# Probabilities times V in smaller steps: one key tile per step, one step per slot, starting a slot earlier

## The chip, the cores and the metric

The kernel runs on one core of a Trainium2 chip. The metric is the device time of one execution in microseconds (us); it is given as the median of three runs. The engines are TensorE (PE, with its weight loads listed apart as PEld), VectorE (DVE), ScalarE (ACT), GpSimd (POOL) and the DMA queues, which SyncE (SP) mostly issues.

## What is computed

Eight sequences of 256 tokens with 128 features pass through four attentions and three feed-forward blocks. Cut to what matters here:

```
x += tanh(g) * attention0(layernorm(x), ctx, ctx)      # 512 keys, 16 heads of 8
x += tanh(g) * moe0(layernorm(x))                      # 8 experts, top 1
z  = layernorm(x)
y  = ln(z + attention1(z, z, z))                       # 256 keys
y  = ln(y + attention2(y, ctx, ctx))                   # 512 keys
y  = ln(y + relu(y @ fc1) @ fc2);  x += tanh(g) * y
u  = x + attention3(rms(x))                            # 256 keys, causal, rope
x += tanh(g) * (u-block: u + moe1(rms(u)))             # 4 experts, top 2
attention:  S = Q K^T * scale;  P = softmax(S);  O = P V   for 16 heads of each of 8 sequences
```

## The kernel before, in words

There are 32 attention batches n (attention 0 for eight sequences, then 1, 2 and 3, named att0 to att3). An attention batch is cut into slots: 16 for 512 keys (one head each, `kt` = 4 key tiles of 128), 8 for 256 keys (two heads each, `kt` = 2). Four heads make a group, so a group is 4 slots (`gs`) with 512 keys and 2 slots with 256.

In a slot TensorE does, in this order, the step E (the transposed scores of the slot's heads with the row maxima folded in, four matmuls, L1654, which ScalarE turns into probabilities by exp, two instructions of 512 columns, L1098, in a ring of nine buffers), and the units S (plain scores of a head some slots ahead, L1619 for 512 keys, L1633 for 256, L1627/L1629 in att3; VectorE takes their maxima, L1288, L1297, L1293). Most slots have two S units; some of att3's have one. Between the S units stand the small products (MISC: q, k, v, transposes "maxT", "ctx", "aT", "proj", "nT") and, in later att0 and early att1 batches, the tiles of the first mixture of experts (L1753, L1762).

The step AV multiplies a group's probabilities with V: per key tile and head one matmul with 128 rows and 32 columns of the array (L1670); four heads fill the four column strips and accumulate in one PSUM bank, `av_ps`. In the trace one such fp32 matmul is two instructions, so 8 matmuls are x16. After a group's last AV step ScalarE copies the bank out (L1102, tile OT), and only then may the next group's first step begin; the first step also waits for the exp of the group's last slot. The same bank serves the second fully connected layer `f.down` (L1783, copied out at L1171), four times in the program.

The order is fixed when the program is built: `body` lists the steps of a batch slot by slot, every engine walks the same list and does its own part. `avs` is how many AV steps a group has. In a slot the AV step is put before the last S unit. Each PE step waits only for what it needs, in order, so whatever stands behind a waiting step waits too. PSUM: three banks for E, three for S (two with 256 keys), the rest for the small products; which step takes which bank is worked out from the same list.

Of the kernel before, what the change touches and what calls it, by code (L numbers as in the profile page):

```python
# [26 lines left out]
NG = HEADS // GH  # L27
# [22 lines left out]
class Att:  # L50
# [3 lines left out]
    def __init__(self, name, keys, own_kv, rope, wo, tail):  # L54
        self.name, self.keys, self.own_kv, self.rope, self.wo, self.tail = name, keys, own_kv, rope, wo, tail
        self.kt = keys // P
        self.slots = HEADS * self.kt * SQ // 1024
        self.hps = HEADS // self.slots
        self.gs = self.slots // NG
        self.lead = 2 * self.gs + 1  # L60
        self.avs = self.kt // 2

    def units(self, s):

# [14 lines left out]
def att(n):  # L79
    return ATTS[n // B]  # L80


def run_of(n):
    return next((lo, hi) for lo, hi in RUNS if lo <= n < hi)
# [9 lines left out]
def post_items(n):  # L94

    a = att(n)
    if n < B and n % HALF == HALF - 1:
        return {4: [("ctx", n, 0)], 5: [("ctx", n, 1)], 6: [("aT", n, None)], 7: [("proj", n, None)],
                9: [("apply", n, None)], 10: [("nT", n, None)]}
    it = {6: [("ctx", n, 0)], 7: [("ctx", n, 1)], 15: [("nT", n, None)]}  # L100
    if a.wo:
        it[8] = [("aT", n, None)]
        it[10 if a.rope else 11] = [("proj", n, None)]
        it[12 if a.rope else 14] = [("apply", n, None)]
    else:
        it[8] = [("resid", n, None)]
        it[10] = [("center", n, None)]
        it[13] = [("apply", n, None)]
    return it


def s_units(n, s, u):

    out = [("S", n, (s, u))]
    a = att(n)
    gs = a.gs
    if u == a.units(s) - 1 and s % gs == gs - 1:
        out.append(("maxsplit", n, s // gs))
    return out
# [170 lines left out]
def opens_half(n):  # L290

    return B <= n < 2 * B and n % HALF == 0
# [12 lines left out]
def body(n, plan):  # L305

    a = att(n)
    lo, hi = run_of(n)
    items = {p: [] for p in range(16)}

    def put(p, *steps):
        items[p] += list(steps)

    put(1, ("maxT", n, 1))
    if n + 1 < hi:
        for hf in range(QUARTERS):
            put((3, 4, 7, 11)[hf] if opens_half(n + 1) else PARTS_AT[hf], ("loadqk", n + 1, hf))
    if n > lo:
        put(2, ("loadres", n - 1, None))
    put(4 if a.rope else 5, ("maxT", n, 2))  # L320
    put(8 if a.rope else 9, ("maxT", n, 3))
    if n + 1 < hi:
        put(13, ("maxT", n + 1, 0))
    if n + 2 < hi and not opens_half(n + 2):
        if n + 2 < 2 * B:
            put(0, ("xapply", n + 2, None))
            put(1, ("xT", n + 2, None))
            if n + 2 >= B:
                put(2, ("xstore", n + 2, None))
        long_k = att(n + 2).kt > 2  # L330
        put(2, ("q", n + 2, None), ("qsplit", n + 2, None))
        put(4, ("k", n + 2, None), ("ksplit", n + 2, 0))
        put(5, ("qstore", n + 2, None))
        if long_k:
            put(6, ("ksplit", n + 2, 1))
        put(10 if long_k else 9, ("kstore", n + 2, None))
    if n > lo:
        for p, st in post_items(n - 1).items():
            put(p, *st)
    if n + 1 < hi:  # L340
        put(12 if a.rope else 10, ("v", n + 1, None))
    if n + 3 < hi:
        if n + 3 < 2 * B and not (n + 3 >= B and (n + 3) % HALF < 2):
            put(8, ("loadx", n + 3, None))
            put(14, ("xstat", n + 3, None))
        if not B <= n + 3 < 2 * B:
            put(12, ("loadin", n + 3, None))
    for k in range(2):
        if 0 <= 2 * (n - WEIGHTS_AT) + k < 2 + 3 * E1:
            put((6, 12)[k], ("weights", n, 2 * (n - WEIGHTS_AT) + k))  # L350
    for p in range(16):
        put(p, *MOE0_ITEMS.get((n, p), ()))
        put(p, *FFN_ITEMS.get((n, p), ()))
    out = []
    per = 16 // a.slots
    for s in range(a.slots):
        ahead = [(m, t, u) for m, t in plan[(n, s)] for u in range(att(m).units(t))]
        units = [s_units(*x) for x in ahead]
        product = []
        if s >= a.gs:  # L360
            product = [("AV", n, (s // a.gs - 1, x)) for x in range(a.avs) if (x + 1) * a.gs // a.avs - 1 == s % a.gs]
        elif n > lo:
            p = att(n - 1)
            product = [("AV", n - 1, (NG - 1, x)) for x in range(p.avs) if (x + 1) * a.gs // p.avs - 1 == s]
        if product:
            units.insert(max(1, len(units) - 1), product)
        tiles = TILE_ITEMS.get((n, s), [])
        units[1:1] = [[st] for st in tiles if st[0] == "m0.h"]
        chunks = [[]]
        for p in range(per * s, per * s + per):  # L370
            for st in items[p] + [st for st in tiles if st[0] != "m0.h" and p % per == per - 1]:
                if st[0] in MISC_KINDS:
                    chunks.append([])
                chunks[-1].append(st)
        out.append(("E", n, s))
        out += weave(units, chunks)
    return out


def weave(units, chunks):  # L380


    rest = chunks[1:]
    if not units:
        units = [[]]
    last, gaps = len(units) - 1, max(1, len(rest) - 1)
    out = list(chunks[0])
    for k, unit in enumerate(units):
        out += unit
        for i, chunk in enumerate(rest):  # L390
            if (2 * i * last + gaps) // (2 * gaps) == k:
                out += chunk
    return out
# [41 lines left out]
def all_steps():  # L435
    out = []
    for lo, hi in RUNS:
        plan = s_plan(lo, hi)
        out += start_steps(plan)
        for n in range(lo, hi):  # L440
            out += body(n, plan)
    return out + moe1_steps()
# [1445 lines left out]
```

## Time and profile before

| | us |
|---|---|
| median of 3 runs | 1217.94 (1216.9 to 1221.68) |
| the profiled execution | 1213.76 |
| its span in the trace | 1211.9 |
| PE busy / DVE busy / ACT busy | 1058.7 / 791.5 / 617.9 |
| mean granted clock of TensorE | 0.941 of full speed |

The span is what the trace covers; about 1.9 us of the profiled execution lie outside it. Busy times of PE are modelled from overlapping matmuls, so that a busy PE may still have short gaps in what it streams; the start times of neighbouring matmuls show these.

### The profile page before, as it was taken

Reading aid. Unit: us, or ns where it says so; the run is one execution under the profiler, and the core shown is the slowest. Engines: PE = TensorE matmul, PEld = TensorE weight load, DVE = VectorE, ACT = ScalarE, POOL = GpSimd, SP = SyncE. Lnnn points to the kernel's source line nnn. Section 1 sums busy time; section 2 is a strip of 40 time slices with the busy share of each in tenths; the row PEclk is TensorE's granted clock in tenths of the full one; section 3 lists DMA queues with packets and bytes.
Section 4 is the critical chain, followed back from the end, with each engine's and each line's share of the span. In section 5 each row is a group of like instructions: output and inputs, shape, how many; then the busy total and the mean of one; then the engine's idle time right before and its main releaser. Section 6 shows DMA issues by size and latency. Waiting matters only on the chain. (4 is left out here: it accounts for less than half of the span.)

```text
span 1211.9 us, 25281 instructions
## 1 busy us (share of the span) xinstructions
PE 1058.7 (87%) x8548; PEld 653.8 (54%) x8548; DVE 791.5 (65%) x1935; ACT 617.9 (51%) x1331; POOL 368.3 (30%) x982
## 2 busy tenths in 40 slices
PE   3999997899887678789799998897989899899998
PEld 1355554576554566445455544444556567656665
DVE  3788888635877213577688869679674766645443
ACT  1477765555663433465477765655644444543221
POOL 3433333221445112542433334213242434200000
PEclk9999999999996788788899998999988989999999
DMA  7556644553444442554666553633434355201000
GB/s 196 157 169 177 174 143 142 183 182 97 126 132 143 155 127 86 161 158 149 212 180 179 151 165 96 179 96 106 123 111 131 115 162 166 88 27 33 20 24 13
DMA packets 173877, 158.76 MB, mean 131 GB/s; under 512 B 13011, under 2 KB 147539, under 8 KB 173395
## 3 DMA queue, kind: packets, MB, share of 16 engines
q1 hardware_dynamic: 169558, 142.03, 39.7%
q0 software_dynamic: 4192, 15.12, 3.9%
q8 instruction: 70, 1.15, 0.4%
q14 instruction: 57, 0.47, 0.1%
HBM read 91.56 MB, written 67.63 MB: 131 GB/s over the span
## 5 line engine op out<-in xcount | busy, mean ns | idle before, releaser
L1098 ACT ACTIVATE prob<-ps 128x512 f32<-128x512 f32 (+1 forms) x768 | 399.3, 579 | 166.1 <-PE ps L1654 123.2
L1288 DVE TENSOR_REDUCE nmax<-ps 128x1 f32<-128x512 f32 x512 | 328.0, 682 | 82.8 <-PE ps L1619 80.6
L1654 PE MATMUL ps<-Qst,Kst 75*128 75x256 bf16 x1408 | 241.6, 282 | 5.9 <-DMA Qst<-mrow 3.0
L1619 PE MATMUL ps<-Kst,Qst 72*128 72x512 bf16 x512 | 195.8, 398 | 24.4 <-DVE nmax L1288 20.8
L1670 PE MATMUL av_ps<-prob,Vx 128*32 128x256 f32 (+1 forms) x3072 | 216.0, 398 | 0.0
L1654 PEld LDWEIGHTS ps<-Qst,Kst 75*128 75x128 bf16 x1408 | 135.7, 100 | 70.8 <-ACT prob L1098 11.5
L1670 PEld LDWEIGHTS av_ps<-prob,Vx 128*32 128x32 f32 x3072 | 92.3, 114 | 66.9 <-issue 37.6
L1020 POOL TENSOR_TENSOR mparts<-nmax,zeros 128x8 bf16<-128x8 f32 x122 | 24.5, 201 | 328.2 <-issue 320.4
L1297 DVE TENSOR_REDUCE nmax<-ps 128x2 f32<-128x512 f32 x128 | 85.7, 686 | 47.3 <-PE ps L1633 46.6
L1102 ACT ACTIVATE OT<-av_ps 128x256 f32<-128x256 f32 x128 | 49.2, 384 | 113.6 <-PE av_ps L1670 113.1
L1619 PEld LDWEIGHTS ps<-Kst,Qst 72*128 72x128 bf16 x512 | 50.2, 99 | 104.7 <-DVE nmax L1288 51.0
L1293 DVE TENSOR_REDUCE nmax<-ps 128x2 f32<-128x512 f32 (+1 forms) x96 | 65.4, 685 | 38.5 <-PE ps L1629 37.7
L1184 ACT ACTIVATE prob<-ps 128x512 f32<-128x512 f32 x48 | 28.7, 597 | 87.2 <-PE ps L1808 87.1
L1633 PE MATMUL ps<-Kst,Qst 72*128 72x256 bf16 x256 | 55.7, 303 | 15.6 <-DVE nmax L1297 11.5
L1159 ACT ACTIVATE m_hid<-ps,wbig 128x256 f32<-128x256 f32 x88 | 35.7, 472 | 57.4 <-PE ps L1762 32.2
L1753 PE MATMUL ps<-FB,wbig 128*128 128x256 f32 x176 | 49.6, 431 | 13.4 <-DMA wbig<-in_w,widx 13.3
L1130 ACT ACTIVATE mrow<-ps 12x256 bf16<-12x256 bf16 x128 | 46.5, 363 | 28.0 <-PE ps L1701 26.2
L1487 DVE TENSOR_TENSOR FB<-ps,wbig 128x256 f32<-128x256 f32 x22 | 9.3, 424 | 75.0 <-PE ps L1762 75.0
L1627 PE MATMUL ps<-Kst,Qst 72*128 72x128 bf16 (+1 forms) x256 | 49.9, 259 | 6.1 <-DVE nmax L1293 6.0
L1570 DVE SCALAR_TENSOR_TENSOR FB<-ps,comb,FB 128x128 f32<-128x128 f32 x64 | 18.0, 344 | 53.9 <-PE ps L1815 53.9
L1815 PEld LDWEIGHTS ps<-wbig,prob 128*128 128x128 f32 x384 | 45.2, 192 | 9.4 <-issue 9.4
L1753 PEld LDWEIGHTS ps<-FB,wbig 128*128 128x128 f32 x176 | 36.1, 216 | 20.7 <-DMA wbig<-in_w,widx 13.9
(198 smaller groups left out, 1673.6 us busy)
## 6 DMA issues: line engine op xcount, KB each, us to landing
k_parts<-kp SPq DMA_DIRECT2D x48, 384.0 KB, 3.4
q_parts<-qp SPq DMA_DIRECT2D x96, 192.0 KB, 2.6
Qst<-q_parts SPq DMA_DIRECT2D x128, 144.0 KB
Kst<-k_parts SPq DMA_DIRECT2D x64, 288.0 KB
k_parts<-kp SPq DMA_DIRECT2D x48, 192.0 KB, 2.6
Kst<-k_parts SPq DMA_DIRECT2D x64, 144.0 KB
ctxT<-in_ctxT SPq DMA_DIRECT2D x16, 256.0 KB, 5.1
xs_rows<-in_blank SPq DMA_DIRECT2D x22, 128.0 KB, 4.0
```

The costliest lines, as they stand in the source:

```text
L1098: act.activation(prob[:, RING_AT[st] % RING, half * 512:half * 512 + w], bank(x)[:, 0:w], ACT.Exp).then_inc(drained(x), 1)
L1102: act.activation(OT[:, n % 2, arg[0], :], av_ps[:, 0:SQ], ACT.Copy).then_inc(av_drained, 1)
L1130: act.activation(mrow[:, arg % 2, :], bank(st)[0:PARTS * GH, :].bitcast(BF16)[:, 0:SQ], ACT.Copy) \
L1288: ve.tensor_reduce(nmax[:, g, u, h % GH:h % GH + 1], bank(st), AX.X, ALU.max, negate=True).then_inc(drained(st), 1)
L1293: ve.tensor_reduce(dst, bank(st).rearrange("p (h k) -> p h k", h=2 if k else GH), AX.X, ALU.max, negate=True).then_inc(drained(st), 1)
L1297: ve.tensor_reduce(nmax[:, g, :, h % GH:h % GH + 1], bank(st).rearrange("p (t k) -> p t k", t=QT), AX.X, ALU.max, negate=True).then_inc(dr ...
L1619: last = pe.matmul(bank(st), Qst[0:ROWS, par, s, u * P:u * P + P], Ks[0:ROWS, par, s, :], start=True, stop=True)
L1627: pe.matmul(o, Qst[0:ROWS, par, h, t * P:t * P + P], Ks[0:ROWS, par, h, 0:w], start=True, stop=False)
L1633: last = pe.matmul(bank(st)[:, t * SQ:t * SQ + SQ], Qst[0:ROWS, par, h, t * P:t * P + P], Ks[0:ROWS, par, h, 0:SQ], start=True, stop=True)
L1654: last = pe.matmul(o, Ks[0:KROWS, par, h, t * P:t * P + P], Qst[0:KROWS, par, h, :], start=True, stop=not a.rope)
L1670: last = pe.matmul(av_ps[VW * hh:VW * hh + VW, SQ - w:SQ], Vx[:, par, t, h, :], prob[:, place, off * SQ:off * SQ + w], start=(t == 0), sto ...
L1753: last = pe.matmul(bank(x)[:, u * TILE:(u + 1) * TILE], w_0[:, arg % WRING, t * P:t * P + P], xs_T[:, arg % 2, :], start=True, stop=True)
```

## The change

Each group has one AV step per key tile (`avs` is `kt` instead of `kt // 2`), with 4 matmuls instead of 8. The rule that places them is rounded up instead of down: the steps of a group with 512 keys stand in the four slots behind the group's last (before: in the second and the fourth of them), with 256 keys in both slots behind it (before: in the second). The last step stays in the slot where it was. The matmuls are the same, 1536 in the program; what stands between them differs. Where an attention with 256 keys follows one with 512, the four steps of the last group stand two and two together.

```diff
@@ class Att
-        self.avs = self.kt // 2
+        self.avs = self.kt
@@ body
         if s >= a.gs:
-            product = [("AV", n, (s // a.gs - 1, x)) for x in range(a.avs) if (x + 1) * a.gs // a.avs - 1 == s % a.gs]
+            product = [("AV", n, (s // a.gs - 1, x)) for x in range(a.avs) if -(-(x + 1) * a.gs // a.avs) - 1 == s % a.gs]
         elif n > lo:
             p = att(n - 1)
-            product = [("AV", n - 1, (NG - 1, x)) for x in range(p.avs) if (x + 1) * a.gs // p.avs - 1 == s]
+            product = [("AV", n - 1, (NG - 1, x)) for x in range(p.avs) if -(-(x + 1) * a.gs // p.avs) - 1 == s]
```

TensorE's order in an att2 batch (slots 1 to 3 of batch 17), before. L1654 is E, L1619 is S, L1670 is AV, L1701 is maxT, L1687 is q:

```order
L1619 MATMUL ps<-Kst,Qst 128x512
L1701 MATMUL ps<-identb,mparts 12x128 x2
L1670 MATMUL av_ps<-prob,Vx 32x256 x8
L1619 MATMUL ps<-Kst,Qst 128x512
L1654 MATMUL ps<-Qst,Kst 128x256 x4
L1619 MATMUL ps<-Kst,Qst 128x512
L1687 MATMUL ps<-inT,wts 128x256
L1619 MATMUL ps<-Kst,Qst 128x512
L1654 MATMUL ps<-Qst,Kst 128x256 x4
L1619 MATMUL ps<-Kst,Qst 128x512
L1670 MATMUL av_ps<-prob,Vx 32x256 x8
```

The same slots on the same engine now:

```order
L1619 MATMUL ps<-Kst,Qst 128x512
L1701 MATMUL ps<-identb,mparts 12x128 x2
L1670 MATMUL av_ps<-prob,Vx 32x256 x4
L1619 MATMUL ps<-Kst,Qst 128x512
L1654 MATMUL ps<-Qst,Kst 128x256 x4
L1619 MATMUL ps<-Kst,Qst 128x512
L1687 MATMUL ps<-inT,wts 128x256
L1670 MATMUL av_ps<-prob,Vx 32x256 x4
L1619 MATMUL ps<-Kst,Qst 128x512
L1654 MATMUL ps<-Qst,Kst 128x256 x4
L1619 MATMUL ps<-Kst,Qst 128x512
L1670 MATMUL av_ps<-prob,Vx 32x256 x4
```

Slot 2 has an AV step of its own, and each step is half as long. Over the program the AV matmuls stand in 379 unbroken runs instead of 192.

TensorE's order around `f.down` (L1783) in batch 19, before:

```order
L1670 MATMUL av_ps<-prob,Vx 32x256 x8
L1619 MATMUL ps<-Kst,Qst 128x512
L1654 MATMUL ps<-Qst,Kst 128x256 x4
L1783 MATMUL av_ps<-prob,wbig 128x512 x4
L1619 MATMUL ps<-Kst,Qst 128x512 x2
L1654 MATMUL ps<-Qst,Kst 128x256 x4
L1619 MATMUL ps<-Kst,Qst 128x512
L1701 MATMUL ps<-identb,mparts 12x128 x2
L1670 MATMUL av_ps<-prob,Vx 32x256 x8
```

The same place now:

```order
L1670 MATMUL av_ps<-prob,Vx 32x256 x4
L1619 MATMUL ps<-Kst,Qst 128x512
L1654 MATMUL ps<-Qst,Kst 128x256 x4
L1783 MATMUL av_ps<-prob,wbig 128x512 x4
L1619 MATMUL ps<-Kst,Qst 128x512
L1670 MATMUL av_ps<-prob,Vx 32x256 x4
L1619 MATMUL ps<-Kst,Qst 128x512
L1654 MATMUL ps<-Qst,Kst 128x256 x4
L1619 MATMUL ps<-Kst,Qst 128x512
L1701 MATMUL ps<-identb,mparts 12x128 x2
L1670 MATMUL av_ps<-prob,Vx 32x256 x4
```

An AV step, which writes the bank that `f.down` has just filled, stands one S unit behind it; before, a whole slot lay between them. The orders of DVE, ACT, POOL and SP are the same row for row, their semaphore waits included.

## Rows read from the trace of the kernel before

**Rows 1.** The page: busy time of each engine; TensorE's granted clock in 40 slices.

```profile
PE 1058.7 (87%) x8548; PEld 653.8 (54%) x8548; DVE 791.5 (65%) x1935; ACT 617.9 (51%) x1331; POOL 368.3 (30%) x982
...
PEclk9999999999996788788899998999988989999999
```

**Rows 2.** Windows: busy us (count) of PE, PEld, DVE, ACT, POOL; clock; DMA.

```profile
42.20:164.70 122.50, 117.18 (x1021) 65.51 (x1019) 103.08 (x231) 85.64 (x178) 44.63 (x128) 1.00 0.58 171
244.00:283.00 39.00, 37.78 (x277) 29.38 (x275) 12.18 (x22) 20.94 (x52) 6.48 (x10) 1.00 0.54 170
...
493.00:613.00 120.00, 98.69 (x777) 55.18 (x776) 84.55 (x197) 63.51 (x139) 48.82 (x135) 0.84 0.61 181
613.00:696.10 83.10, 81.02 (x748) 45.15 (x747) 72.98 (x148) 62.19 (x130) 30.98 (x90) 1.00 0.56 167
...
733.80:770.30 36.50, 31.12 (x261) 16.89 (x259) 33.15 (x84) 21.66 (x44) 14.33 (x41) 0.91 0.47 141
...
885.40:1072.00 186.60, 166.29 (x1813) 120.82 (x1810) 123.05 (x350) 87.53 (x215) 68.33 (x211) 0.92 0.43 128
```

**Rows 3.** Waits in 613 to 696.1: who waited for whom, us, times, longest.

```profile
DVE nmax L1288 <- PE ps L1619: 7.6, 18, 0.8
...
PE ps L1619 <- DVE nmax L1288: 1.5, 6, 0.4
```

**Rows 4.** Timeline of TensorE in batch 17: start, us, what, xcount.

```profile
640.30 0.60 PE L1619 MATMUL ps<-Kst,Qst 72*128 72x512 bf16 x2
640.74 0.65 PE L1654 MATMUL ps<-Qst,Kst 75*128 75x256 bf16 x4
...
644.15 0.60 PE L1654 MATMUL ps<-Qst,Kst 75*128 75x256 bf16 x4
644.59 0.38 PE L1619 MATMUL ps<-Kst,Qst 72*128 72x512 bf16 x1
644.90 1.07 PE L1670 MATMUL av_ps<-prob,Vx 128*32 128x256 f32 x16
645.90 0.39 PE L1619 MATMUL ps<-Kst,Qst 72*128 72x512 bf16 x1
646.13 0.60 PE L1654 MATMUL ps<-Qst,Kst 75*128 75x256 bf16 x4
```

**Rows 5.** The page's groups: busy, mean ns, idle before them and its releaser.

```profile
L1288 DVE TENSOR_REDUCE nmax<-ps 128x1 f32<-128x512 f32 x512 | 328.0, 682 | 82.8 <-PE ps L1619 80.6
...
L1670 PE MATMUL av_ps<-prob,Vx 128*32 128x256 f32 (+1 forms) x3072 | 216.0, 398 | 0.0
...
L1670 PEld LDWEIGHTS av_ps<-prob,Vx 128*32 128x32 f32 x3072 | 92.3, 114 | 66.9 <-issue 37.6
...
L1619 PEld LDWEIGHTS ps<-Kst,Qst 72*128 72x128 bf16 x512 | 50.2, 99 | 104.7 <-DVE nmax L1288 51.0
```

**Rows 6.** Timeline of ACT in the same slots as rows 4.

```profile
644.94 1.09 ACT L1098 ACTIVATE prob<-ps 128x512 f32<-128x512 f32 x2 [0.17 <-ACT qk L1111]
646.03 0.38 ACT L1102 ACTIVATE OT<-av_ps 128x256 f32<-128x256 f32 x1
```

**Rows 7.** Timeline around the first `f.down`, all engines.

```profile
723.13 3.70 PE L1783 MATMUL av_ps<-prob,wbig 128*128 128x512 f32 x8 [0.37 <-ACT OT L1102]
...
726.66 0.60 PE L1619 MATMUL ps<-Kst,Qst 72*128 72x512 bf16 x2
...
726.86 0.69 ACT L1171 ACTIVATE FB<-av_ps,cols 128x512 f32<-128x512 f32 x1 [2.81 <-PE av_ps L1783]
...
727.08 1.89 DVE L1288 TENSOR_REDUCE nmax<-ps 128x1 f32<-128x512 f32 x3 [4.07 <-PE ps L1619]
```

**Rows 8.** Waits over the whole span.

```profile
DVE nmax L1288 <- PE ps L1619: 80.6, 87, 7.2
...
DVE nmax L1297 <- PE ps L1633: 46.6, 40, 5.3
...
DVE nmax L1293 <- PE ps L1629: 37.7, 42, 5.7
```

## The prediction, made before the changed kernel was run

> **What bounds the kernel now.** I read the busy times first. TensorE is busy 1058.7 of 1211.9 us, VectorE 791.5, ScalarE 617.9, GpSimd 368.3 [rows 1]. An average says little in a program of so many stages, so I cut it into windows [rows 2]. In the plain 512-key batches (42 to 164.7 and 613 to 696.1) TensorE is busy 117.2 of 122.5 and 81.0 of 83.1 us; in the tiles of the first experts (244 to 283) 37.8 of 39. In the 256-key batches it has more room: 98.7 of 120 (attention 1) and 166.3 of 186.6 (attention 3). Batch 20 (733.8 to 770.3) is VectorE's: 33.2 of 36.5 us against TensorE's 31.1.
>
> In the plain batches VectorE is close behind: 73.0 of 83.1 us. The waits tell which of the two is late. VectorE waited 7.6 us for scores, TensorE 1.5 us for a score bank to be read [rows 3]. So TensorE is what is late, by a little; both have almost no room.
>
> The timeline shows how a slot is made up [rows 4]. Two S matmuls take 0.60 us where one takes 0.38, so the next starts 0.22 us after the last. E begins at 644.15 and the S behind it at 644.59, 0.44 us. A slot without AV is thus 0.44 + 2 x 0.22 = 0.88 us of TensorE; the slot with AV, from E at 644.15 to E at 646.13, is 1.98. The mean of 1.43 stands against 2 x 0.682 = 1.36 us of VectorE's maxima [rows 5] plus its other work. Light and heavy slots alternate, and the three score banks even them out.
>
> **What an AV run costs.** S starts at 644.59 and AV at 644.90, 0.31 us later instead of 0.22: entering costs 0.09. The run of 16 instructions takes 1.07 us. They go four at a time, one per column strip, so it is one matmul's 0.38 us and three further rounds of (1.07 - 0.38) / 3 = 0.23. The next S starts 1.00 us after the run began, 0.07 before its last end [rows 4]. A run of 4 matmuls is two rounds: 0.38 + 0.23 = 0.61, less 0.07 is 0.54. With the entry, 8 matmuls in one run are 1.00 + 0.09 = 1.09 us and in two runs 2 x (0.54 + 0.09) = 1.26. Each further run costs 0.17 us at full clock.
>
> The Trainium skill speaks against the change at this place. "TensorE: Matmul & The Clock Gate", section "Part 3: Packing small matmuls — row/col tiling", says that a weight load overlaps running matmuls only if it goes to other row groups; AV takes all 128 rows and 32 columns, its neighbours all rows too. By that rule each further run would pay one load of either kind, 0.114 and 0.099 us [rows 5], 0.21 us and 39 us over the kernel; the trace agrees in kind, with 0.17.
>
> **The change part by part.** Matmuls, bytes and the other engines' orders stay. Every group with 512 keys has two more runs and every group with 256 keys one: 16 batches x 8 + 16 x 4 = 192, less 5 where two steps stand together (two in each of the two passages from 512 to 256 keys, one at the end). That is the 187 of 379 - 192. 187 x 0.17 = 31.8 us more of TensorE's time. What of it reaches the end depends on the stretch:
>
> - Plain batches 0 to 3, 7 and 16 to 18: 64 runs, 10.9 us. Their idle TensorE is 5.3 us in four batches and 2.1 in three [rows 2]. Some of that idle is S waiting for a bank in the slots that had no AV, and an AV step before it covers that wait. I take 7 tenths on the path: 7.6 us. Bounds 3 and 10.9.
> - Batches 5 and 6 with expert tiles: 16 runs, 2.7 us, little idle TensorE; 7 tenths, 1.9. Bounds 1 and 2.7.
> - Batches 19, 21 and 23 with the fully connected layers: 24 runs, 4.1 us. VectorE starves there (4.07 us before 727.08 [rows 7]), so TensorE sets the pace: 2.9. Bounds 2 and 4.1.
> - Batches 4, 20, 22: 24 runs, 4.1 us, VectorE's; nothing. Bounds 0 and 2.
> - The 256-key batches: 59 runs, 10.0 us. TensorE stands idle there 21.3 of 120 and 20.3 of 186.6 us; three tenths, 3.0. Bounds 0 and 7.
>
> **The new wait.** The first step of a group is one slot earlier and needs the exp of the slot before and the copy of `av_ps`. In batch 17 the last exp of slot 3 ends at 644.94 + 1.09 = 646.03 and the copy at 646.41 [rows 6]; the slot's E started at 646.13 and takes 0.44, so S starts at 646.57 and AV 0.31 later at 646.88: 0.47 us of room. With half the matmuls in slot 3 the copy is ready sooner, by up to 0.46, and TensorE also arrives sooner by the same. I take nothing; at 0.1 us for each of 128 groups it would be 13 us, a high bound that I find unlikely.
>
> Behind `f.down` there is no such room. Its copy runs 726.86 to 727.55; the S before starts at 726.66, so AV could start at 726.97 and must wait until about 727.6 [rows 7]. Queued behind it are the other S unit, which VectorE is starving for, and the next E, for which ScalarE is busy anyway. 0.65 x 4 = 2.6 us, bounds 0 and 4.
>
> **What evenness gives back.** A slot that was heavy loses 0.46 us between its two S units, so VectorE is fed more evenly. VectorE waited for scores 80.6, 46.6 and 37.7 us in all [rows 8], but much of it in expert tiles and `f.down`, which stay. In the plain batches it can't help beyond what I left off the path above. In the 256-key batches and in 4, 20 and 22 it can: I take about a tenth of the 84.3 us of L1297 and L1293, 8 us, bounds 0 and 25.
>
> Sum: 7.6 + 1.9 + 2.9 + 0 + 3.0 + 2.6 - 8 = 10 us. The profiled execution of 1213.76 would become 1223.8. The median of the runs shown stands 4.2 us higher, and I predict against it: 1217.94 + 10 = 1228.
>
> **Rivals.**
> - *Evenness wins.* Alternation of 0.88 and 1.98 us slots starves VectorE in every heavy slot: 18 waits in 83 us [rows 3]. If steady feeding takes 7.6 us down to 2 there and the same share elsewhere, with TensorE's own waits gone as well, up to 25 us come back in the 256-key batches and the plain ones lose only 3. Against it: a starved VectorE costs nothing while TensorE is late. It decides if TensorE's streaming in plain batches has more gaps than the 2.1 us seen. Time: 10 + 8 - 25 - 5 is -12, about 1206. Chance 0.17.
> - *It cancels.* The lower bounds of the costs (3 + 1 + 2) against 6 of the gain: 1218. Chance 0.2.
> - *Every run is on the path.* 31.8 + 2.6 and nothing given back: 1252. Needs TensorE to be the bound everywhere, against its 21.3 us idle in attention 1 [rows 2]. Chance 0.06.
> - *The clock moves.* From 493 to 613 the granted clock averages 0.84 and from 885.4 to 1072 0.92: about 38 and 30 us at 1.2 instead of 2.4 GHz. It falls there because TensorE waits in bursts. If AV work in the light slots keeps it up in half of these, up to half of 34 us comes back, and about 1211 is reached; if other gaps appear it may be lost the same way, 1240. Chance 0.07, half each way. The Trainium skill ("TensorE: Matmul & The Clock Gate", "Part 1: The HAM clock gate") says that the throttled state is the default and activity lifts it; taken alone it would favour the first half, and no row here shows AV's placing to move it.
> - *The forecast*, 1221 to 1240, chance 0.5.
>
> **How the numbers follow.** About 0.5% (6 us) is what a measurement of this kernel can tell from no change. Faster: 0.17 and 0.02 of the clock, 0.19. Same: 0.2 of cancelling and 0.06 of the forecast's lower edge, 0.26. Slower: the rest, 0.55. The range of 1209 to 1243 takes in cancelling, the mild part of evenness and the bounds of the costs; outside lie the strong win below and the all-on-path case above, together about 2 in 10. The forecast's own range is 1221 to 1240.
>
> **What would show it.** The changed kernel's timeline of a plain slot should show each slot near 1.5 us instead of 0.9 and 2.0; S to AV 0.31 and AV run of x8 with the next S 0.54 after its start. Batches 16 to 18 should take about 3 us more than 83.1. VectorE's waits for L1619 should be shorter and more frequent. Behind `f.down` a wait of L1670 on ACT of about 0.6 us should stand four times. The prediction is wrong if the plain batches get shorter, if x8 runs follow each other without the 0.17 us, or if att1 and att3 shrink by more than 8 us.

## The result, and the profile after

| | before | after |
|---|---|---|
| median | 1218.18 us (5 runs) | 1251.42 us (5 runs) |
| the same comparison again, beside the experiments | 1221.32 us (17 runs) | 1246.75 us (6 runs) |

The ratio is 1.0235 with an interval of 1.0172 to 1.0298, and 1.0284 (1.0198 to 1.0371) the second time. The medians are of all executions; the ratios leave out those that stand more than 1.5% above the fastest of their kernel. The change makes the kernel 2 to 3% slower. The direction was forecast; 1228 us and the range up to 1243 were too low. The profiled execution has a span of 1243.2 us, 31.3 more than before.

The page of the changed kernel, answering to [rows 1] and [rows 5]:

```profile
PE 1103.0 (89%) x8548; PEld 635.7 (51%) x8548; DVE 798.0 (64%) x1935; ACT 621.7 (50%) x1331; POOL 368.4 (30%) x982
...
PEclk9999997899997889887799998898997999899999
...
L1288 DVE TENSOR_REDUCE nmax<-ps 128x1 f32<-128x512 f32 x512 | 332.2, 685 | 104.0 <-PE ps L1619 102.5
L1670 PE MATMUL av_ps<-prob,Vx 128*32 128x256 f32 (+1 forms) x3072 | 259.5, 404 | 3.7 <-ACT FB L1171 2.7
```

The matmuls are as many as before, and TensorE is busy 44 us longer, all but a little of it at L1670 (259.5 against 216.0 us). VectorE waits 22 us more for the scores of the long attentions in this pair of traces, although they come more evenly. The granted clock averages 0.924 instead of 0.941.

TensorE's timeline of batch 17, answering to [rows 4]:

```profile
655.84 0.60 PE L1654 MATMUL ps<-Qst,Kst 75*128 75x256 bf16 x4
656.28 0.38 PE L1619 MATMUL ps<-Kst,Qst 72*128 72x512 bf16 x1
656.59 0.64 PE L1670 MATMUL av_ps<-prob,Vx 128*32 128x256 f32 x8
657.16 0.39 PE L1619 MATMUL ps<-Kst,Qst 72*128 72x512 bf16 x1
657.39 0.60 PE L1654 MATMUL ps<-Qst,Kst 75*128 75x256 bf16 x4
```

The slot is 1.55 us from E to E, where light and heavy slots had 0.88 and 1.98, 1.43 in the mean. I had forecast a slot near 1.5. S to AV is still 0.31 us. The run of x8 takes 0.64 us and the next S starts 0.57 after it began. So 8 matmuls in two runs are 2 x (0.57 + 0.09) = 1.32 us against 1.09 in one: a further run costs 0.23 us, not the 0.17 that I worked out. The median of the 68 runs of x8 that stand between S units at full clock in this trace is the same 0.57, and that of the 20 runs of x16 in the trace of before 1.00. The starts of the single matmuls in that trace, merged in [rows 4], tell where my 0.54 went wrong: the second round starts 0.24 us after the first, each later one 0.22 after the last, and the next S 0.33 after the last round began. What a run pays beyond its rounds lies at its two ends, and I had left part of it in the rounds.

Windows of the changed kernel: batches 16 to 18 (answering to 613 to 696.1 of [rows 2]) and batch 20.

```profile
628.90:713.50 84.60, 83.99 (x748) 41.48 (x746) 73.66 (x148) 62.19 (x129) 31.32 (x92) 1.00 0.56 165
753.10:793.90 40.80, 36.11 (x260) 16.82 (x259) 33.83 (x84) 21.74 (x44) 14.41 (x41) 0.83 0.42 127
```

These three plain batches, at full clock throughout, are 1.5 us longer in 83, half of the 3 us that I had given as a sign, and TensorE stands idle for 0.6 us of them where it did for 2.1. Batch 20 is 4.4 us longer, with the clock at 0.83 where it was 0.91, and I had expected nothing of it.

The waits in 628.9 to 713.5, answering to [rows 3]:

```profile
DVE nmax L1288 <- PE ps L1619: 8.3, 19, 1.1
...
PE ps L1619 <- DVE nmax L1288: 0.4, 2, 0.2
```

TensorE's own waits are nearly gone. VectorE's should have become shorter and more frequent, and did not (19 up to 1.1 us, where there were 18 up to 0.8): TensorE is now simply late. Over the whole span, the waits of the 256-key attentions, answering to [rows 8]:

```profile
DVE nmax L1297 <- PE ps L1633: 46.7, 53, 4.4
...
DVE nmax L1293 <- PE ps L1629: 40.9, 38, 5.5
```

Together they are 87.6 us where there were 84.3. I had taken 8 us of these waits as what evenness gives back. The other trace of the changed kernel has 91.1, a second one of the kernel before 88.6 (9.1 of them without a releaser in the profile). They did not shrink.

The place behind the first `f.down`, answering to [rows 7]:

```profile
745.03 0.38 PE L1619 MATMUL ps<-Kst,Qst 72*128 72x512 bf16 x1
745.24 0.69 ACT L1171 ACTIVATE FB<-av_ps,cols 128x512 f32<-128x512 f32 x1 [2.81 <-PE av_ps L1783]
...
746.07 0.64 PE L1670 MATMUL av_ps<-prob,Vx 128*32 128x256 f32 x8 [0.65 <-ACT FB L1171]
...
747.07 0.69 DVE L1288 TENSOR_REDUCE nmax<-ps 128x1 f32<-128x512 f32 x1 [0.92 <-PE ps L1619]
```

AV waits 0.65 us for the copy, and VectorE starves 0.92 us behind it.

**By stretch.** Batch lengths, from a batch's first exp to the next one's, and in brackets the us of them at 1.2 GHz, from the clock record of one trace each:

| batches | before | before again | after | after again |
|---|---|---|---|---|
| plain: 1, 2, 3, 16, 17, 18 | 175.1 (0) | 175.6 (0) | 180.3 (0) | 179.9 (0) |
| 19, 21, 23 | 114.6 (3) | 116.6 (7) | 120.1 (3) | 117.2 (0) |
| 4, 20, 22 | 112.4 (7) | 114.1 (15) | 119.8 (29) | 117.0 (28) |
| 5, 6 | 116.2 (7) | 124.9 (19) | 122.8 (19) | 124.6 (27) |
| attention 1 | 265.5 (92) | 268.6 (99) | 267.7 (96) | 272.0 (99) |
| attention 3 | 186.5 (31) | 184.2 (21) | 189.9 (38) | 185.2 (27) |

The plain batches repeat within 0.5 us and show the change's own cost, 4.3 to 5.2 us; batches 1 to 3 bear 3.7 of it in the first pair and 16 to 18 the 1.5 above. The others scatter, in part with the clock: batches 5 and 6 took 116 and 125 us in two traces of the same kernel. Before the second trace of the kernel before I had set down that over 20 us at the low clock in batches 4, 20 and 22 would forbid putting their rise down to the change. It had 15, but see e5_short_only below.

**Taking the clock out.** Each timed execution comes with its span and mean clock c. There are two levels, 1.2 and 2.4 GHz, so (1 - c) x 2 x span is the time at the low one. Over 129 executions in 16 series, one for each kernel of the tables and the kernel before again in each of four comparisons, a fit with one constant for each series gives 0.34 us of span for each us at the low clock (standard error 0.02, scatter 3.9 us). This splits a difference between two kernels in two: their own parts, taken at the same low-clock time, and what the difference in low-clock time adds. The kernel before has to be the one timed in the same comparison: its constants on the four chips, taken at 150 us of low clock, lie between 1218 and 1225 us, and its mean low-clock time between 149 and 173. The columns "own part" and "low clock" below go by this; the standard error of an own part is about 2 us.

| kernel | runs of AV | ratio (interval) | own part over before's | low clock (before's beside it) |
|---|---|---|---|---|
| before | 192 | 1 | 0 | 149 to 173 |
| after, first comparison | 379 | 1.0235 (1.0172 to 1.0298) | not known | 199 (not known) |
| after, second | 379 | 1.0284 (1.0198 to 1.0371) | +11 | 202 (149) |
| e1_split | 375 | 1.0306 (1.016 to 1.0453) | +22 | 196 (158) |
| e2_early | 190 | 1.0136 (0.9995 to 1.0278) | +6 | 173 (158) |
| e3_one_run | 128 | 1.023 (1.0096 to 1.0364) | +12 | 188 (158) |
| e4_long_only | 316 | 1.026 (1.0113 to 1.0408) | +10 | 188 (158) |
| e5_short_only | 255 | 1.0078 (1.0036 to 1.012) | 0 | 176 (149) |
| e6_av_last | 192 | 1.0166 (1.009 to 1.0243) | +8 | 173 (149) |
| e7_fdown_apart | 375 | 1.0194 (1.0104 to 1.0285) | +5 | 192 (149) |
| e8_fill | 379 | 1.0116 (1.003 to 1.0201) | +16 | 163 (173) |
| e9_before_fill | 192 | 0.9953 (0.9919 to 0.9986) | +11 | 119 (173) |
| e10_half_fill | 192 | 0.9957 (0.9919 to 0.9994) | +5 | 121 (152) |

For the change: 11 us of its own and 52 x 0.34 = 18 us by the clock. Together they are the 29 us between the mean spans (1248.0 and 1219.2); that they add up is how the split is made and no test of it. That the slope, found within kernels, also prices the difference between kernels is assumed.

### The profile page after: what moved, and what is told of

Its sections match the earlier page's. It is cut to its first block and busy times, and to the rows that moved or that the text cites. A ratio compares the mean times of both kernels' runs of the same rounds, so it can differ in the third digit from the quotient of the medians.

```text
span 1243.2 us, 25281 instructions
## 1 busy us (share of the span) xinstructions
PE 1103.0 (89%) x8548; PEld 635.7 (51%) x8548; DVE 798.0 (64%) x1935; ACT 621.7 (50%) x1331; POOL 368.4 (30%) x982
## 5 line engine op out<-in xcount | busy, mean ns | idle before, releaser
L1098 ACT ACTIVATE prob<-ps 128x512 f32<-128x512 f32 (+1 forms) x768 | 404.0, 578 | 230.9 <-PE ps L1654 183.0
L1288 DVE TENSOR_REDUCE nmax<-ps 128x1 f32<-128x512 f32 x512 | 332.2, 685 | 104.0 <-PE ps L1619 102.5
L1670 PE MATMUL av_ps<-prob,Vx 128*32 128x256 f32 (+1 forms) x3072 | 259.5, 404 | 3.7 <-ACT FB L1171 2.7
L1654 PE MATMUL ps<-Qst,Kst 75*128 75x256 bf16 x1408 | 247.3, 289 | 2.0 <-DMA Qst<-mrow 0.9
L1619 PE MATMUL ps<-Kst,Qst 72*128 72x512 bf16 x512 | 206.7, 408 | 17.4 <-DVE nmax L1288 14.1
L1654 PEld LDWEIGHTS ps<-Qst,Kst 75*128 75x128 bf16 x1408 | 141.8, 103 | 60.0 <-issue 12.9
L1619 PEld LDWEIGHTS ps<-Kst,Qst 72*128 72x128 bf16 x512 | 50.5, 99 | 136.9 <-issue 85.5
L1297 DVE TENSOR_REDUCE nmax<-ps 128x2 f32<-128x512 f32 x128 | 86.4, 687 | 47.5 <-PE ps L1633 46.7
L1670 PEld LDWEIGHTS av_ps<-prob,Vx 128*32 128x32 f32 x3072 | 69.5, 111 | 88.9 <-issue 81.5
L1293 DVE TENSOR_REDUCE nmax<-ps 128x2 f32<-128x512 f32 (+1 forms) x96 | 65.0, 685 | 41.4 <-PE ps L1629 40.9
L1633 PE MATMUL ps<-Kst,Qst 72*128 72x256 bf16 x256 | 58.3, 315 | 13.6 <-DVE nmax L1297 10.9
L1701 PE MATMUL ps<-identb,mparts 128*12 128x128 bf16 x256 | 37.1, 229 | 12.8 <-POOL mparts L1026 9.0
```

The costliest lines, as they stand in the source:

```text
L1098: act.activation(prob[:, RING_AT[st] % RING, half * 512:half * 512 + w], bank(x)[:, 0:w], ACT.Exp).then_inc(drained(x), 1)
L1288: ve.tensor_reduce(nmax[:, g, u, h % GH:h % GH + 1], bank(st), AX.X, ALU.max, negate=True).then_inc(drained(st), 1)
L1293: ve.tensor_reduce(dst, bank(st).rearrange("p (h k) -> p h k", h=2 if k else GH), AX.X, ALU.max, negate=True).then_inc(drained(st), 1)
L1297: ve.tensor_reduce(nmax[:, g, :, h % GH:h % GH + 1], bank(st).rearrange("p (t k) -> p t k", t=QT), AX.X, ALU.max, negate=True).then_inc(dr ...
L1619: last = pe.matmul(bank(st), Qst[0:ROWS, par, s, u * P:u * P + P], Ks[0:ROWS, par, s, :], start=True, stop=True)
L1633: last = pe.matmul(bank(st)[:, t * SQ:t * SQ + SQ], Qst[0:ROWS, par, h, t * P:t * P + P], Ks[0:ROWS, par, h, 0:SQ], start=True, stop=True)
```

## The experiments

My theory after the result: each further run is paid, and the clock follows. The rival: the places are at fault, the first step standing a slot earlier. A second rival: it is the clock's own scatter.

**e1_split: the number of runs alone.**

```diff
-        self.avs = self.kt // 2
+        self.avs = self.kt
-  if (x + 1) * a.gs // a.avs - 1 == s % a.gs
+  if (x // 2 + 1) * a.gs // (a.avs // 2) - 1 == s % a.gs      # likewise for p
-            units.insert(max(1, len(units) - 1), product)
+            units.insert(max(1, len(units) - 1), product[:1])
+            units[-1] = units[-1] + product[1:]
```

The AV steps stand in the slots of before, but each is cut in two, with the last S unit between the halves.

> The slots of before (AV work in every second slot, none in the others), but each AV step of 8 matmuls is cut into two of 4 with the last S unit between them: 375 unbroken runs of AV matmuls instead of 192, and the uneven slots stay. If the number of runs is the cause (0.17 us each on TensorE, nearly all on the path, and a lower clock behind it), it takes 1240 to 1252 us. If the new places of the steps are the cause, it stays within 1212 to 1226 us.

Measured: 1258.7 us, 1.0306, above my range for this theory. Runs alone, at the old places, cost as much as the change or more. Its timeline shows two runs in one slot, the first of them in two lines, with a small transpose between:

```profile
689.72 0.42 PE L1671 MATMUL av_ps<-prob,Vx 128*32 128x256 f32 x3
...
689.82 0.59 PE L1671 MATMUL av_ps<-prob,Vx 128*32 128x256 f32 x5
690.35 0.39 PE L1620 MATMUL ps<-Kst,Qst 72*128 72x512 bf16 x1
690.67 0.64 PE L1671 MATMUL av_ps<-prob,Vx 128*32 128x256 f32 x8
691.24 0.61 PE L1655 MATMUL ps<-Qst,Kst 75*128 75x256 bf16 x4
```

Batches 17 and 18 take 29.15 and 29.35 us at full clock, against 27.77 and 27.96 before: 1.38 and 1.39 us for 8 more runs, 0.17 each. On the engine a run costs 0.23; that waits which it fills pay the rest is likely and not shown. In the changed kernel the same batches take 28.80 and 28.57 (28.37 and 28.56 again): the even places give back 0.4 to 0.8 of the 1.4 us. So in these batches the count of runs is what costs, and the new places don't add to it: they take some of it away.

**e2_early: the places alone.**

```diff
-  if (x + 1) * a.gs // a.avs - 1 == s % a.gs
+  if max(0, (x + 1) * a.gs // a.avs - 2) == s % a.gs          # likewise for p
```

> Steps of 8 matmuls as before (190 runs), but each one slot earlier, so that the first stands in the slot behind the group's last, as in the changed kernel. If the number of runs is the cause, it takes 1212 to 1226 us (and about 2.6 us of waiting behind f.down). If the earlier first step is the cause, 1230 to 1250 us.

Measured: 1237.74 us, 1.0136 with an interval that just holds 1. Own part +6, low clock 173 beside 158, which is inside the scatter of its four executions. The total lies in the range that I had given for the earlier first step: there are two runs fewer than before, and yet some 6 us of its own. In its order the AV steps stand in slots 0, 2, 4 and so on, where q, k, v also stand:

```profile
699.79 0.38 PE L1619 MATMUL ps<-Kst,Qst 72*128 72x512 bf16 x1
700.03 0.70 PE L1687 MATMUL ps<-inT,wts 128*128 128x256 f32 x2
700.65 1.07 PE L1670 MATMUL av_ps<-prob,Vx 128*32 128x256 f32 x16
701.66 0.39 PE L1619 MATMUL ps<-Kst,Qst 72*128 72x512 bf16 x1
```

1.87 us lie between two S units here; VectorE's two maxima of that slot take 1.36. In the kernel before, q, k and v stand in slots without AV. That this is what the 6 us are was not tested by itself.

**e3_one_run: fewer runs.** Groups with 512 keys do their 16 matmuls in one run.

```diff
-        self.avs = self.kt // 2
+        self.avs = 1
```

> Groups with 512 keys do all 16 matmuls in one run, in the slot where their last step stood: 128 runs instead of 192. If each run costs 0.17 us on the path, 64 runs fewer give 11 us back: 1203 to 1211 us. If evenness matters more, the slots with 16 matmuls starve VectorE and ScalarE: 1222 to 1240 us.

Measured: 1245.56 us, 1.023, above both of my ranges. The count of runs is not the whole of it. The timeline of a run of 16 matmuls (x32):

```profile
667.70 0.38 PE L1619 MATMUL ps<-Kst,Qst 72*128 72x512 bf16 x1
668.01 1.93 PE L1670 MATMUL av_ps<-prob,Vx 128*32 128x256 f32 x32
669.87 0.39 PE L1619 MATMUL ps<-Kst,Qst 72*128 72x512 bf16 x1
```

It is 2.17 us from S to S, and VectorE has three score banks, 2.05 us of work. The kernel before seems to lie between two costs: more runs are paid on TensorE, and longer ones starve VectorE, which waits 16.0 us for L1619 in batches 16 to 18 of this trace, where it waited 7.6. (10 us of these batches are at the low clock here, none before.)

**e4_long_only and e5_short_only: the change in one kind of attention.**

```diff
-        self.avs = self.kt
+        self.avs = self.kt if self.kt == 4 else 1      # e4_long_only
+        self.avs = 2                                    # e5_short_only
```

> The change for the attentions with 512 keys alone, those with 256 keys as before: 316 runs, 124 more than before. By the number of runs with all of them on the path 124 x 0.17 = 21 us, and some of the lost clock: 1238 to 1250 us. If the loss sits in the 256-key attentions, under 1226 us.

> The change for the attentions with 256 keys alone, those with 512 keys as before: 255 runs of AV matmuls, 63 more than before. If runs are paid one by one, 63 x 0.17 = 11 us at most, less what the idle TensorE of these attentions hides: 1220 to 1234 us, and less than the long attentions cost. If evenness pays where TensorE has room (VectorE waits 84 us there in the kernel before), it is 1205 to 1216 us.

Measured: 1245.29 us, 1.026, and 1229.41 us, 1.0078. The long attentions carry the change's own cost (+10 us for 124 runs). In the short ones 63 runs cost nothing of their own (0, with a standard error of 1.6 us). Idle TensorE may hide them, 21.3 of 120 us in attention 1 before; VectorE's waits for L1297 and L1293 are 89.4 us here, 84.3 and 88.6 before, so evenness gave nothing back that shows. The 0.8% that is left comes with 26 us more at the low clock.

**after_again: the changed kernel beside these.**

> The changed kernel again, with its placing untouched, on one chip with the kernels of this group. The runs so far fit span = kernel's own part + 0.34 us for each us at the low clock. If the loss has two parts, its own part is some 17 us over the kernel before and its low-clock time some 40 us longer (another 14 us): ratio 1.018 to 1.030. If the first comparison was mostly a difference of chips, the ratio is under 1.012.

Measured: 1246.75 us, 1.0284, with both kernels on one chip; low clock 202 us beside 149. The loss isn't one of chips. The own part is 11 us instead of the 17 that the runs up to then had given.

**e6_av_last: VectorE fed sooner.** The kernel before with AV behind the last S unit.

```diff
-            units.insert(max(1, len(units) - 1), product)
+            units.append(product)
```

> The kernel before with each AV step behind the slot's last S unit instead of ahead of it, so that VectorE gets its second score bank 1 us sooner in the slots with AV work; 192 runs as before, and as many entries from full-array matmuls. If VectorE's waits in those slots count, 1205 to 1214 us and under 4 us of waiting for L1619 in the plain 512-key batches 16 to 18 (7.6 before). If TensorE is late anyway, it is within 0.5 percent of the kernel before.

Measured: 1238.56 us, 1.0166. It is slower, which neither side expected, with 24 us more at the low clock. In its batches 16 to 18 (624.8 to 710.7) the wait did not fall:

```profile
DVE nmax L1288 <- PE ps L1619: 10.0, 17, 1.0
```

The AV run now joins the next E, 1.00 and 0.44 us in which no score is made. It looks as if moving the block by one place trades one starved stretch for another. Why the total loses 8 us of its own stays open.

**e7_fdown_apart: the wait behind f.down.** In `body` of the changed kernel (`held` starts empty in each batch):

```diff
+        if any(st[0] == "f.down" for p in range(per * s, per * s + per) for st in items[p]):
+            held, product = product, []
+        else:
+            held, product = [], held + product
```

> The changed kernel, but the AV step that stands right behind f.down waits one slot and joins the next, four times in the program (375 runs instead of 379). If the wait for the copy of av_ps is the 2.7 us that the trace shows at L1670 behind ACT FB, batches 19, 21 and 23 are each 0.7 to 1.0 us shorter than in the changed kernel and the idle time of L1670 before it falls from 3.7 to about 1; the total is 3 us shorter, inside the noise. If the wait only moved elsewhere, the batches stay at 39.6, 42.1 and 38.4 us.

Measured: 1241.64 us, 1.0194, which is 5 us below after_again and inside the noise. Batches 19, 21 and 23 take 38.62, 41.55 and 36.73 us, against 39.57, 42.12 and 38.37, but after_again has 39.76, 40.00 and 37.48 with the wait in place. The wait is gone:

```profile
L1675 PE MATMUL av_ps<-prob,Vx 128*32 128x256 f32 (+1 forms) x3072 | 261.4, 408 | 1.0 <-ACT OT L1107 0.9
```

L1675 is this kernel's L1670; its idle time is 1.0 us instead of 3.7. Batches 19 and 23, at full clock in both, are 1.1 and 0.8 us below after_again; batch 21 is not, and had 3.4 us at the low clock. The wait of 2.7 us is real and small.

**e8_fill, e9_before_fill, e10_half_fill: is it the clock?** A matmul whose result is overwritten stands ahead of each E half:

```diff
+                        if n in (4, 20, 22):                       # e8_fill, on the changed kernel
+                        if n in (4, 20, 22) or B <= n < 2 * B:     # e9 and e10, on the kernel before
+                            pe.matmul(bank(x)[:, 0:SQ], identb[:, :], maskb[...],   # e10: 0:P, 128 columns
+                                      start=True, stop=True)
```

> The changed kernel with one more bf16 matmul of 128x256 ahead of each E half in batches 4, 20 and 22 only, its result overwritten: 96 more matmuls, about 0.11 us each, 10 us of TensorE's time where it stands idle for 9 to 11 us a batch. If TensorE's low activity there is what lets the clock fall, the low-clock time of these three batches goes from 28 us to under 12 and the batches from 117 to 120 us down to 112 to 118. If the clock falls with the waits whatever is put between them, low-clock time stays over 20 us and the batches take 122 to 130 us.

> The kernel before with the same filling matmuls in batches 4, 20, 22 and in all eight of attention 1 (224 of them, 24 us of TensorE's time). Those stretches hold about 100 of its 150 us at the low clock. If filling keeps the clock up, the low-clock time falls to under 100 us and the total to 1203 to 1217 us. If not, the fillers are paid: 1225 to 1245 us.

> As e9_before_fill, with fillers of 128 columns instead of 256 (about 0.05 us each, 12 us of TensorE's time instead of 24). If even short fillers keep the clock up, the low-clock time stays near 120 us and the total is 5 to 8 us below e9's ratio of 0.995: ratio 0.986 to 0.992. If the clock needs the longer ones, the low-clock time is back over 145 us and the ratio 1.000 to 1.010.

Windows of the changed kernel ahead of and in a fall of the clock in batch 20:

```profile
743.00:746.40 3.40, 2.75 (x15) 0.93 (x13) 0.69 (x1) 0.69 (x1) 0.00 (x0) 1.00 0.58 163
746.40:749.80 3.40, 3.32 (x34) 1.70 (x26) 2.56 (x5) 1.33 (x3) 0.00 (x0) 1.00 0.02 5
749.80:753.20 3.40, 3.22 (x31) 1.61 (x30) 3.22 (x12) 2.72 (x6) 1.05 (x2) 1.00 0.01 4
753.20:756.60 3.40, 2.75 (x27) 0.93 (x25) 3.22 (x10) 2.54 (x5) 1.04 (x5) 1.00 0.59 188
756.60:760.00 3.40, 2.60 (x9) 1.41 (x8) 3.21 (x6) 1.09 (x2) 0.00 (x0) 0.61 0.40 111
760.00:763.40 3.40, 3.40 (x23) 1.14 (x22) 2.34 (x7) 1.56 (x3) 2.29 (x5) 0.50 0.25 81
```

TensorE's busy time sinks from 3.3 to 2.7 us while VectorE is busy 3.2 of 3.4, then the clock is at 1.2 GHz for 10 us. The first row warns against reading more into it: TensorE is as little busy there, and no fall follows. Batches 4, 20 and 22 of the changed kernel, then of e8_fill:

```profile
169.50:209.00 39.50, 33.79 (x282) 17.49 (x281) 30.77 (x82) 22.02 (x46) 11.67 (x34) 0.94 0.42 123
753.30:794.10 40.80, 36.11 (x260) 16.88 (x258) 33.83 (x84) 21.80 (x44) 14.23 (x41) 0.83 0.42 127
836.30:875.80 39.50, 34.86 (x264) 16.77 (x262) 35.36 (x90) 20.68 (x43) 12.85 (x37) 0.87 0.36 110
```

```profile
170.60:210.50 39.90, 36.64 (x314) 20.29 (x311) 30.51 (x81) 22.19 (x46) 11.20 (x33) 0.96 0.41 122
762.20:800.60 38.40, 34.52 (x292) 18.53 (x289) 33.85 (x84) 21.92 (x44) 14.49 (x41) 0.96 0.45 135
840.60:879.50 38.90, 33.86 (x295) 17.96 (x293) 35.15 (x90) 21.04 (x42) 12.78 (x36) 1.00 0.37 111
```

Filled, their low-clock time is 7 us instead of 29 (28 again) and their length 117.2 instead of 119.8 (117.0 again), as forecast. The total is 1242.64 us, 1.0116, where the changed kernel had 1.0235 and 1.0284; the intervals overlap, and the changed kernel was not timed on that chip. Its low-clock time is 163 us beside 173 of the kernel before, so the rise that the change brings is gone, as far as chips can be compared, and the own part is +16 instead of +11. The same fillers on the kernel before, in attention 1 too. That attention first without and then with them, with 92 and 61 us at the low clock:

```profile
347.40:613.00 265.60, 211.89 (x1575) 135.67 (x1573) 147.46 (x370) 122.47 (x280) 93.32 (x225) 0.83 0.50 152
```

```profile
358.90:623.20 264.30, 215.93 (x1701) 143.83 (x1699) 148.00 (x370) 123.30 (x279) 92.82 (x224) 0.88 0.51 153
```

One trace of each tells little of the length, as the second trace of the kernel before has 268.6. Over the timed executions the low-clock time falls from 173 to 119 us (e9) and from 152 to 121 (e10), each beside the kernel before on the same chip, with a standard error of 5 us. The totals are 1225.66 us beside 1234.35 (ratio 0.9953) and 1215.90 beside 1220.83 (ratio 0.9957). e9 was to bring the low-clock time under 100 us and the total to 1203 to 1217; neither came. e10 was to reach 0.986 to 0.992, and didn't. The long fillers cost 11 us of own part and save 54 at the low clock, the short ones cost 5 and save 31: both come out at some 5 to 7 us of gain, less than a percent, and which is better these runs can't tell. What they do show is that more TensorE work in these stretches keeps the clock up.

## Why the prediction was wrong

- *What bounds the kernel*: right. TensorE stands idle for 0.6 of 84.6 us in the plain batches now.
- *The cost of a further run*, 0.17 us: the right mechanism, mis-sized. 0.23 us on the engine; 0.17 is what reached the end in e1_split's batches 17 and 18.
- *Plain batches, 7.6 us for 64 runs*: right. Six of the eight, with 8 runs each but for one, lost 4.3 to 5.2 us; 7.6 for 64 runs is 5.6 for their 47.
- *Batches 5 and 6, 1.9 us*: not told. They took 116 and 125 us before and 123 and 125 after.
- *Batches 19, 21, 23, 2.9 us, and f.down, 2.6*: 5.5 us in the first pair of traces and 0.6 in the second. The wait was 2.7 us, as forecast.
- *The new wait elsewhere, nothing*: right. All that L1670 waits besides `f.down` is 1.0 us.
- *Batches 4, 20, 22, nothing*: they took 3 to 7 us more, with 28 us at the low clock against 7 and 15. That can't be put down to their AV steps: e5_short_only, where the order of these batches is the old one, had 44 us of it in its one trace and took 123.1.
- *The 256-key batches, 3.0 less 8 for evenness*: wrong. They were to gain 5 us, with help from batches 4, 20 and 22, and cost nothing and gained nothing of their own (e5_short_only). The waits of VectorE that were to shrink by 8 us are 87.6 and 91.1, where they were 84.3 and 88.6.
- *Sum*: 10 us were forecast and the own part is 11, with a standard error of 2. That is partly luck: the terms of the long attentions add up to 15 us and e4_long_only has 10; the missing gain of 5 in the short ones makes up for it.
- *The step that failed* is the rival "the clock moves". I gave it 0.07, half each way, and so left it out of the sum, at nothing. It went one way: low-clock time 149 to 202 us, some 18 us of span, and 1218 + 11 + 18 = 1247 is near what was measured (1246.75 and 1251.42). [rows 2] had shown that 68 us in two stretches were at the low clock, so that a change of the order could move much, but not which way it would go. The bad side was also priced too low: half of 34 us on top of 1228 is 1245, not the 1240 that I wrote, and outside my range. All reorderings tried here, whatever their run count, have more low-clock time than the kernel before beside them, by 15 to 52 us; for e1, e2 and e4, with four executions each, that is within or near the scatter. Where fillers were added it fell, or didn't rise.
- The case "every run is on the path", 1252 us, has the measured time and the wrong reason: 11 us of own cost are far from its 34.

By the rule of the Trainium skill that I drew on ("TensorE: Matmul & The Clock Gate", "Part 3: Packing small matmuls — row/col tiling") my estimate for a further run is 0.21 us; the trace has 0.23 on the engine, nearer to it than to my 0.17. As a rule for every matmul the trace doesn't bear it out. The rounds of an AV run stand 0.22 us apart, but the four E matmuls, also of 256 columns and each with a load of its own into the same rows, 0.11. The neighbours of AV take 72 and 75 rows, not all as I wrote.

What stays open: why these reorderings lead to more time at the low clock. The fillers show that TensorE work added in these stretches takes low-clock time away. That thinner AV runs lower the activity where it matters is only argued, and the 44 us of e5_short_only in batches with the old order speak against a purely local cause.

## What to carry to other kernels

Split a block of packed matmuls only if the entry and exit of each further run (0.23 us here) is less than what evenness returns; where the engine was 97% busy it wasn't. Where part of a kernel runs at a clock below full, sum the change's own terms and then price the clock apart, from the scatter of repeated executions (0.34 us of span per us at the low clock here), and don't take it as even because its sign is unknown. Compare such parts only between kernels timed on one chip: the kernel before alone differs by 6 us of own part and 23 us of low-clock time between chips. And a matmul whose result nobody needs can be worth its time where TensorE waits in short pieces, by half a percent here.

## What the hardware showed beyond that

- Two bf16 matmuls of 128 columns a slot, ahead of E, in the 256-key attention 1 and batches 4, 20 and 22, took 31 us off the low-clock time (152 to 121) for 5 us of own part.
- Executions of one unchanged kernel lay between 1207.6 and 1241.5 us over the four chips used. The low-clock time goes along with about two thirds of that variance (the mean clock was 0.925 to 0.948 in the first of these series).
- In a column-packed run of fp32 matmuls of 256 columns, a further round costs 0.22 us, and the ends cost more: 0.57 us to the next S for two rounds, 1.00 for four and 1.87 for eight (e3_one_run).
